# A q/k product ahead of a batch's first scores, five other moves in one order, and logits in 16 products

## The reference

```
x = layernorm(x + attn(x))                       # x: 8 x 512 x 256
normed = x * rsqrt(mean(x^2) + 1e-8) * norm_weight
shared = relu(normed @ sw1 + sb1) @ sw2 + sb2    # 256 -> 1024 -> 256
probs  = sigmoid(normed @ router_w.T)            # 8 experts
scores, idx = top_k(probs, 2);  w = scores / (sum(scores) + 1e-6)
routed = sum over the two chosen e of w * (relu(normed @ ew1[e] + eb1[e]) @ ew2[e] + eb2[e])
out = layernorm(x + shared + routed)
```

## Time and profile before

| | us |
|---|---|
| median of 3 runs | 939.65 (939.44 to 940.9) |
| the profiled execution's own time | 943.1 |
| its span (first to last instruction) | 941.4 |
| PE, PEld, DVE, ACT, POOL busy | 882.9, 699.4, 583.6, 613.7, 428.9 |

### The profile page before, as it was taken

How to read it: one execution, slowest core, us unless ns; L and a number is a source line. 1 busy time by engine, 2 the same in 40 slices (tenths; PEclk the granted TensorE clock), 3 DMA queues, 4 the chain that set the end, 5 groups by cost and what they waited for, 6 DMA issues and landing times.

```text
span 941.4 us, 26124 instructions
## 1 busy us (share of the span) xinstructions
PE 882.9 (94%) x9049; PEld 699.4 (74%) x9050; DVE 583.6 (62%) x1206; ACT 613.7 (65%) x1061; POOL 428.9 (46%) x602
## 2 busy tenths in 40 slices
PE   4778999999999979999999999999999999999997
PEld 1444556565556647888888999998999989898886
DVE  8653778988989747783554544444444432437976
ACT  4678988888988867343665555556655454666774
POOL 5342454778868627571234434344434344512311
PEclk8789999999999999999999999999999999999999
DMA  5120231415312256467883122121212111238751
GB/s 178 68 90 1 68 102 52 145 45 158 114 47 100 100 203 217 147 224 275 261 269 111 56 68 68 46 73 51 68 48 76 46 58 48 76 118 284 229 168 56
DMA packets 67601, 108.56 MB, mean 115 GB/s; under 512 B 7648, under 2 KB 45920, under 8 KB 67392
## 3 DMA queue, kind: packets, MB, share of 16 engines
q1 hardware_dynamic: 50144, 73.12, 23.9%
q10 hardware_dynamic: 10896, 16.40, 6.0%
q0 software_dynamic: 6480, 17.97, 5.3%
HBM read 64.48 MB, written 42.98 MB: 114 GB/s over the span
## 4 chain that ended last, share of the span: by engine, by line
PE 63%; POOL 11%; issue 8%; ACT 8%; DVE 6%; DMA 2%; another core or an unknown queue 1%; ACTq 0%; DVEq 0%; POOLq 0%; SPq 0%
PE yb L1916 24%; PE hb L1897 24%; ACT prob L884 4%; PE pv_bank L1681 3%; PE hb L1747 3%; POOL rsum L712 2%; PE tr L1767 1%; POOL xg_rows L753 1%; POOL rsum L709 1%; PE slot L1655 1%; POOL nat L727 1%; POOL vv L736 1%; DMA rs<-resid 1%; PE yb L1784 1%
## 5 line engine op out<-in xcount | busy, mean ns | idle before, releaser
L1056 ACT ACTIVATE hf<-hb,b 128x256 f32<-128x256 f32 (+1 forms) x392 | 154.6, 453 | 197.1 <-PE hb L1897 173.8
L1897 PE MATMUL hb<-xgT,wts 128*128 128x256 f16 (+1 forms) x1872 | 213.3, 263 | 1.9 <-ACT hf L1056 1.6
L1916 PE MATMUL yb<-wts,hh 128*128 x1704 | 210.6, 273 | 0.7 <-DVE hh L1485 0.6
L1485 DVE TENSOR_TENSOR hh<-hf,hh 128x1024 f16<-128x1024 f32 (+1 forms) x98 | 119.0, 1217 | 132.2 <-ACT hh L1061 107.3
L1897 PEld LDWEIGHTS hb<-xgT,wts 128*128 x1872 | 181.2, 98 | 21.3 <-issue 1.6
L819 POOL DMA_INDIRECT y_tok<-yb,dest x71 | 78.2, 1101 | 226.4 <-DVE yb L1497 209.6
L1916 PEld LDWEIGHTS yb<-wts,hh 128*128 128x128 f16 x1704 | 166.3, 98 | 19.7 <-DVE hh L1485 1.0
L884 ACT ACTIVATE prob<-slot 128x1024 f32<-128x1024 f32 x160 | 156.5, 1042 | 36.4 <-PE slot L1668 34.3
L1061 ACT ACTIVATE hh<-hf 128x1024 f16<-128x1024 f32 (+1 forms) x98 | 97.6, 996 | 3.1
L753 POOL DMA_INDIRECT xg_rows<-xnh,sl_i x64 | 74.9, 1170 | 15.4 <-issue 13.1
L1681 PE MATMUL pv_bank<-prob,vst 128*32 128x512 f32 (+3 forms) x1024 | 75.6, 436 | 0.5 <-ACT prob L884 0.5
(11 more groups left out here) (250 smaller groups left out, 1438.4 us busy)
## 6 DMA issues: line engine op xcount, KB each, us to landing
wts<-in_w_all SPq DMA_DIRECT2D x27, 512.0 KB
wts<-y_tok SPq DMA_DIRECT2D x32, 256.0 KB, 4.8
xg<-xg_rows ACTq DMA_DIRECT2D x30, 264.0 KB
xTf<-in_xT SPq DMA_DIRECT2D x8, 512.0 KB
stage<-in_w_all SPq DMA_DIRECT2D x8, 512.0 KB
w_split<-chunk_hl SPq DMA_DIRECT2D x8, 512.0 KB, 3.0
xin<-in_x SPq DMA_DIRECT2D x8, 512.0 KB
resid<-y SPq DMA_DIRECT2D x16, 256.0 KB
```

Source lines behind the costliest of these rows:

```text
L1056: act.activation(hf[:, c, 0:size], hb[c // 2][:, (c % 2) * TT:(c % 2) * TT + size], ACT.Relu, bias=bias, scale=1.0 / WS).then_inc(S("relu_ ...
L1485: dve.tensor_tensor(hh[:, par, 1, cs, 0:size], hf[:, cs, 0:size], hh[:, par, 0, cs, 0:size], ALU.subtract).then_inc(S("h_lo"), 1)
L1897: ins = pe.matmul(hb[hc // 2][:, (hc % 2) * TT:(hc % 2) * TT + size], weights(e, c, w, hc * P, P), xgT[:, par, x * DC + c, 0:size], start= ...
L1916: ins = pe.matmul(bank, hh[:, par, x, hc, P * j:P * j + P], weights(e, DC + hc * D // CH, w, hc * D % CH, D), start=(n == 0), stop=(n == H ...
```

## The change

```diff
-XN_ROWS = (38, 43)
+XN_ROWS = (40, 43)
-SPACED = (58, 60, 64, 66)
+SPACED = (58, 63, 65, 66)
-CHUNK_AT = 6
-CHUNK_GAP = 18
+CHUNK_POS = (10, 30, 50, 70, 90, 110, 130, 144)
+CHUNK_LOW = 2
...
-    return [k for k in range(len(CHUNKS)) if CHUNK_AT + k * CHUNK_GAP == g]
+    return [k for k in range(len(CHUNKS)) if CHUNK_POS[k] == g]
...
-        wrout = sb("wrout", [P, 2, DC, NE], F16)
+        wrout = sb("wrout", [P, DC, 2, NE], F16)
...
-                        act.activation(ex[:], mx[:, :, 0:2], ACT.Exp, scale=-1.0).then_inc(S("ex_ready"), 1)
+                        act.activation(ex[:], mx[:, :, 0:2], ACT.Exp, scale=-1.0 / RS).then_inc(S("ex_ready"), 1)
...
-                    then(dve.tensor_scalar(lg[:].rearrange("p t e -> p (t e)"), mc[:, 0:NT * NE], 1.0 / RS, None, ALU.mult),
+                    then(dve.tensor_reduce(lg[:], mc[:, 0:2 * NT * NE].rearrange("p (t y e) -> p t e y", y=2, e=NE),
+                                           AX.X, ALU.add),
...
-                    for c, _ in due(SPLIT_X, g - 1):
+                    for c, _ in due(SPLIT_X, g - 3):
...
-                    for k in chunk_due(g - 1):
+                    for k in chunk_due(g - CHUNK_LOW):
...
                 def step(g):
+                    for c, t in due(QK, g):
+                        if c >= 2 and position(QK, c, t) % NPOS == 0:
+                            pe.wait_ge(S("xT_lo"), c + NT)
+                            pe.wait_ge(S("ma_free"), NTH["qk", c, t])
+                            product(qk_bank(c, t), c, t, slice(0, 2 * D)).then_inc(S("qk_done"), 1)
                     for c, p in due(UNITS, g):
...
                     for c, t in due(QK, g):
+                        if c >= 2 and position(QK, c, t) % NPOS == 0:
+                            continue
...
-                        four = [(x, y, k) for k in range(DC) for x in range(2) for y in range(2)]
+                        both_halves = [(x, k) for k in range(DC) for x in range(2)]
                         for t in range(NT):
-                            for n, (x, y, k) in enumerate(four):
-                                last = pe.matmul(mc[:, t * NE:(t + 1) * NE], xnT[:, t // 2, x * DC + k, t % 2, :], wrout[:, y, k, :],
-                                                 start=(n == 0), stop=(n == len(four) - 1))
+                            for n, (x, k) in enumerate(both_halves):
+                                last = pe.matmul(mc[:, 2 * t * NE:2 * (t + 1) * NE], xnT[:, t // 2, x * DC + k, t % 2, :],
+                                                 wrout[:, k, :, :].rearrange("p y e -> p (y e)"),
+                                                 start=(n == 0), stop=(n == len(both_halves) - 1))
```

More of the change, by code:

```diff
@@ L152 @@
 N_RAW = N_CHUNKS - len(CHUNKS)
-assert CHUNK_AT + (len(CHUNKS) - 1) * CHUNK_GAP <= EARLY_IN - 7 and len(CHUNKS) % 2 == 0
+assert len(CHUNK_POS) == len(CHUNKS) and CHUNK_POS[-1] + CHUNK_LOW <= EARLY_IN - 6 and len(CHUNKS) % 2 == 0
 def rows_due(g):
@@ L861, in split_more @@
                     act.activation(wproj[:, 0, :, :], stage[:, :, w:w + D], ACT.Copy, scale=WS).then_inc(S("w_hi"), 1)
-                    act.activation(wrout[:, 0, :, :], stage[:, :, w + D:], ACT.Copy, scale=RS).then_inc(S("w_hi"), 1)
+                    act.activation(wrout[:, :, 0, :], stage[:, :, w + D:], ACT.Copy, scale=RS).then_inc(S("w_hi"), 1)
                 act.wait_ge(S("vst_one"), 1)
@@ L1154, in low_more @@
                     low(2, wproj, w, w + D, WS)
-                    low(3, wrout, w + D, w + D + NE, RS)
+                    low(3, wrout[:].rearrange("p k y e -> p y k e"), w + D, w + D + NE, RS)
                 dve.wait_ge(S("const_ready"), 2)
```

## The result

The changed kernel takes 931.61 us (median of 4 runs, 930.3 to 932.83), the kernel before 939.55 (4 runs, 938.7 to 940.9) on the same chip: ratio 0.990, 95% interval 0.9884 to 0.9915. The forecast was 931.0 in 926 to 937.5. Its profiled execution took 932.83, span 931.1.

A forecast was written before the change was run, and what follows sets the result against it. PE was taken to set the pace in b2 to b6. The terms, 3.0 + 2.6 + 2.5 + 1.2 + 2.6 - 3.2 = 8.7 us, came off the median 939.65 to give 931.0, range 926 to 937.5.

The forecast's parts named there:

- What bounds the kernel: PE sets the pace in b2 to b6; in b7 it waits for exponentials.
- a saving on PE comes off the end one for one: Time saved in the batches shortens the whole run equally, since the next stages start from PE's own order.
- The q/k product ahead: At a batch's start the product, needing only `ma`, begins 0.50 us earlier; six batches, 3.0 us gained.
- The waits for POOL: Rows' norm and scatter move back, so PE's four waits for doubled halves go; 2.6 us gained.
- The waits for DVE: x's low half goes behind the division PE waits for, removing four waits; 2.5 us gained.
- Chunks on ACT: High halves move behind position 10, away from exponentials PE waits for; 1.2 us gained, nothing in b7.
- Logits: 16 matmuls of 16 columns replace 32 of 8, saving 0.43 us in each of six batches; 2.6 us.
- The new wait: The chunk's low half before L1233 makes PE wait at L1719 in four batches; 3.2 us lost.
- the first, ACT takes over: ACT doesn't catch up the later exponentials, six batches lose 0.7 us; gain 4.7, time 935; chance 0.21.
- The second: DVE can't get below about 40 us a batch, waits only change names; 938 to 941, no change; chance 0.09.
- The third: Slower: behind the logits DVE, lengthened by POOL, makes PE wait 2.7 us in six batches; 944 us; chance 0.06.
- The fourth: More gain: b7's idle 3.63 us vanishes, or no wait appears at L1719; with both 924.2 us; chance 0.06.

The follow-up runs named there:

- u_qk: The changed kernel with only the q/k product put back behind the two score units and their masks; 938.34 us, ratio 0.9923 to the kernel before.
- low14_uqk: low14 with the q/k product of a batch's start put back behind that batch's first score step; 938.37 us, ratio 0.9925 to the kernel before.
- low14: The changed kernel with the chunk's low half at position 14 instead of 12, behind `y`, last chunk at 143; 932.06 us, ratio 0.9854.
- u_rows: The changed kernel with the first rows' norm and the scatters of tiles 1 and 2 at their old places; 940.22 us, ratio 0.9937.
- u_split: The changed kernel with the split of x's low half on DVE back at its old place; 939.29 us, ratio 0.9942.
- after_again: The changed kernel itself, unchanged, run again on the last chip; 938.00 us, ratio 0.9919 to the kernel before.
- u_lg: The changed kernel with the logits back to 32 products of 8 columns and the scaling for the reduction; 939.72 us, ratio 0.9940.
- only_lg: The kernel before with only the logits changed, to 16 products; 943.79 us, ratio 0.9985.
- best: low14 with the q/k copy and square ahead of the copy of a pv bank in ACT's step; 931.02 us, ratio 0.9847.
- after: The changed kernel as first measured and profiled, with all edits; 931.61 us, ratio 0.990 to the kernel before.
- tiny_low: The changed kernel with the low halves of chunks 2 to 6 cut to 32 of 1024 columns; 935.32 us, ratio 0.9886.
- u_chunk: The changed kernel with the eight chunks at their old positions, low halves one position behind the high halves; 938.78 us, ratio 0.9920.

## Why the prediction was right, and where it wasn't

The total was right, 931.6 against 931.0, but some of that is luck: the parts that can be pinned to the change (b1 to b6 and the shared stage) sum to 6.4, not 8.7, and about 1.5 of the medians' 7.9 comes from elsewhere. Of the 6.4, b6's 0.78 rests on one profile.

- What bounds the kernel: PE in b2 to b6, right. That a saving on PE comes off the end one for one failed in b3 to b5.
- **The q/k product ahead**, 3.0: 0.36 in b1 and b2 (u_qk), 0.36 in the others only without the wait for `y` (low14_uqk). 0.50 was too high, and low14_uqk against low14 shows where it went in b3: the product starts 0.44 earlier than the scores would (5.84 against 6.28 after the period's start), and then the masks take 0.43 instead of 0.34 up to the next row, probabilities times values, which now stand right behind them. 0.36 is left. So the order of the same matmuls has a price of its own, 0.09 here.
- **The waits for POOL**, 2.6: 2.3 (u_rows, with 0.58 in b6). Right, though not all of a wait could go: behind POOL's half stands ACT's square, and 0.24 a batch is left for it. The list shows 1.3 for POOL and not under 1; that is a new wait, from the logits.
- **The waits for DVE**, 2.5: the wait is gone as forecast, but the split alone is worth 1.0 in b2 to b5 (u_split), since the next wait of the same chain takes the rest.
- **Chunks on ACT**, 1.2: the waits for exponentials tell of it. b2's wait for exponentials of 0.89 went, b6's 0.47 became 0.59, in after_again about 1.3. I put it at some 0.9. b7 can't be read.
- **Logits**, 2.6: the width was right (31 ns for 16 columns against 27 for 8, 0.38 a batch saved), the step that PE's saving counts was not: nothing in b2 to b5 (u_lg, only_lg), 0.2 to 0.4 in the shared stage. The turning two positions on waits for the square of the position-12 product, and behind that for POOL's half (best). I had asked only what stands behind the logits on PE, not what the next turning waits for.
- **The new wait**, -3.2: 0.76, 0.72 and 0.76 in b3 to b5, none in b2, 2.2 in all, within the forecast's 0.5 to 1.1. Its price is higher than itself, 2.9 (low14). The size of the wait came out by two errors that cancel: in b4 DVE ends `y` 6.52 after the logits (232.45 less 225.93) where 5.93 was forecast, since it starts on them late and the low half takes 1.80; and PE comes for the bank 5.94 after them, not 5.39, half of the difference by the 0.27 at the turning. That b2 has no wait has a cause too: in b3 to b5 POOL's two copies stand behind a scatter (227.28 to 228.26 in b4) and meet the low half; in b2 no scatter stands there, the copies are over, and the low half takes 1.21. The forecast counted 0.8 lost and the q/k product, DVE waits and logits won in full; in truth this wait is where the product's gain ended and most of the DVE waits', and the logits' had gone at the turning before it.

Of the rivals the first, ACT takes over, is out: the waits for exponentials are 0.7 up to b6, and 4 was its sign. The second came nearest in kind: in b5 the whole gain is 0.17. Not because DVE can't go below 40, low14 does, but because of one operation in a bad place. The third's mechanism was there, with 2.2 of waiting in place of its 16.2. The fourth's first half, b7's stand-still gone, happened in the profiled execution and gave 2.7 of its 10.3. What makes up the rest of the medians' 7.9 over the 6.4, b7 or the opening (75.64 here, 74.16 in best, 74.55 in only_lg with the order of before), stays open.

## What to carry to other kernels

An edit that makes the bounding engine faster is worth its time only up to the next point where that engine meets another one's chain; look up the next such waits in order, their slack included, before multiplying a saving by the number of batches. Work that an engine has to do at some time belongs behind the results that others wait for: moving 1.8 us by two positions was worth 2.9 us in three batches, cutting it out almost wholly no more. When periods repeat to 0.03 us and the ratios' intervals are 3 to 6 us wide, undo one edit at a time and read the periods.

## What the runs showed of the hardware

DVE and POOL hold each other up. Columns: count, duration min/median/max in ns, starts; the chunk's low half on DVE in after, then in low14:

```profile
L1470 DVE SCALAR_TENSOR_TENSOR chunk_hl<-stage,chunk_hl x7: 1212/1451/1805, 107.1 to 328.5; 128x1024 f16<-128x1024 f32 x7
```

```profile
L1470 DVE SCALAR_TENSOR_TENSOR chunk_hl<-stage,chunk_hl x7: 1217/1218/1241, 114.3 to 328.3; 128x1024 f16<-128x1024 f32 x7
```

Beside the 1.80 in after's b4 stand POOL's two copies of the doubling and then its swap:

```profile
228.27 0.41 POOL L727 COPY nat<-nat 128x256 f32<-128x256 f32 x1
228.61 0.40 POOL L728 COPY nat<-nat 128x256 f32<-128x256 f32 x1
228.97 1.72 POOL L709 TENSOR_TENSOR rsum<-qk_raw,stab 128x256 f32<-128x256 f32 x1
230.66 1.16 POOL L712 TENSOR_TENSOR rsum<-qk_raw,stab 128x256 f32<-128x256 f32 x1
```

tiny_low tells which of them holds DVE. Its low half of 32 columns, in b4, and POOL beside it:

```profile
226.88 0.77 DVE L1471 SCALAR_TENSOR_TENSOR chunk_hl<-stage,chunk_hl 128x32 f16<-128x32 f32 x1
```

```profile
226.82 0.41 POOL L727 COPY nat<-nat 128x256 f32<-128x256 f32 x1
227.16 0.40 POOL L728 COPY nat<-nat 128x256 f32<-128x256 f32 x1
227.53 0.72 POOL L709 TENSOR_TENSOR rsum<-qk_raw,stab 128x256 f32<-128x256 f32 x1
```

Alone it takes 0.18 (b2), here 0.77, as long as the copies run: 0.59 more. In after the low half takes 1.80 instead of 1.22, 0.58 more, behind the same two copies. The copies keep their 0.40. The swap L709, 0.72 beside the small operation, takes 1.72 behind the large one: it is now POOL that waits. By these rows the one that comes first keeps its time. The Trainium skill, SBUF — State Buffer, section "Who interferes with whom", says that a DVE instruction with two SBUF inputs contends with a GpSimd instruction that reads SBUF, over a shared port pair that it calls an exclusive lock; these rows agree.

PE's clock fell to half for 3.4 us (in u_split for 6.8) once or twice between the opening and the routed stage in 10 of 14 profiles. Windows of after_again; the column behind POOL is the granted clock:

```profile
303.40:306.80 3.40, 2.09 (x36) 1.51 (x34) 3.23 (x6) 2.20 (x3) 2.79 (x3) 0.99 0.13 45
306.80:310.20 3.40, 3.40 (x27) 2.83 (x26) 3.08 (x16) 3.38 (x7) 3.25 (x5) 0.50 0.11 40
```

0.50 is the lower level, 1.2 GHz. Before it fell PE had waited 0.78 and 0.52 us for exponentials; in u_chunk's b4 it had waited the 2.16. b6 is 39.47 there against 37.21 in after: PE is idle for 1.99 against 1.25 and busy for 37.49 against 35.96, so the half clock cost about 1.5 and the gaps 0.7. It happens to the same order of work in one run and not in another. The changed kernel's runs have a mean granted clock of 0.986 to 0.990 beside its median of 931.61 and of 0.982 to 0.985 beside its 938.0. The kernel before is longer by 6.1 there too, so these 6 us belong to the runs and not to the change.
